# Layer 0's expert block in one order with the last units of its main attention

## What is computed

```python
x = x + gate_attn * attention(h)                  # main attention adds onto x, 256 tokens a unit
h = layernorm(x) * (1 + scale) + shift
inh = sigmoid(h @ Wr / temperature)               # 8 logits for each token
in_zone = (inh >= LO) & (inh <= 0.5)
distance = abs(inh - 1/e)
w  = exp(-distance / 0.1) * in_zone
fb = exp(-distance / 0.3) * top2_mask             # used where no expert is in the zone
weights = normalised(where(sum(w) < 1e-8, normalised(fb), w))
y = sum_e weights[:, e] * ((silu(h @ Wg[e]) * (h @ Wu[e])) @ Wd[e])
x = x + gate_ffn * y
```

## Time and profile before

| what | value |
|---|---|
| time, median of 3 runs | 1442.34 us (1441.42 to 1442.78) |
| the profiled execution's own time | 1450.17 us |
| its span, first to last instruction | 1448.0 us |
| mean granted TensorE clock | 0.951 of full speed |
| busy in the span: PE, DVE, ACT, POOL | 1313.8, 761.2, 761.9, 470.0 us |
| stretch from 828.6 to 1052.6 us: PE busy, granted clock | 180.02 of 224.00 us, 0.89 |
| first up product of the experts starts | 860.80 us |
| the four additions of one unit onto x; the statistics of four tiles behind them (DVE) | 1.66 us; 2.0 us (857.52 to 859.51 us) |
| from one expert's first up product to the next one's, experts 2 to 7 | 17.8 us |
| an expert's weights, issue to landing (768 KB) | 4.4 us |
| layer 1's attention weights (1024 KB): issue, time to landing | 875.35 us, 4.8 us |

### The profile page before, as it was taken

One profiled execution on the slowest core, in us unless ns is written; L12 is line 12 of the kernel. 1 busy time (PEld: TensorE's weight loads), 2 busy tenths in 40 slices (PEclk: granted clock), 3 DMA queues, 4 the chain that ended last, 5 costly groups with the idle time before them and its releaser, 6 DMA issues.

```text
span 1448.0 us, 21051 instructions
## 1 busy us (share of the span) xinstructions
PE 1313.8 (91%) x7838; PEld 884.5 (61%) x7838; DVE 761.2 (53%) x1233; ACT 761.9 (53%) x1424; POOL 470.0 (32%) x430
## 2 busy tenths in 40 slices
PE   6889999889999999999999867899658998779998
PEld 3633333347777776777777656788634444468997
DVE  4488877324454454454544634444337764354555
ACT  3457776655555555555555544233124767526553
POOL 4260054217465646555563002233300000013221
PEclk9989999999999999999999988899869999869999
DMA  7770000000000000000001011111037100011110
GB/s 274 182 174 1 1 16 8 9 0 23 15 15 15 16 23 11 19 16 23 8 23 52 1 44 43 38 45 44 1 92 166 25 1 1 1 48 52 46 43 30
DMA packets 27144, 59.57 MB, mean 41 GB/s; under 512 B 5986, under 2 KB 13410, under 8 KB 25954
## 3 DMA queue, kind: packets, MB, share of 16 engines
q1 hardware_dynamic: 27044, 58.24, 14.6%
HBM read 41.44 MB, written 8.39 MB: 34 GB/s over the span
## 4 chain that ended last, share of the span: by engine, by line
PE 81%; DVE 7%; ACT 5%; issue 3%; POOL 1%; DMA 1%; SPq 0%; ACTq 0%; DVEq 0%; POOLq 0%
PE bank L1525 8%; PE bank L1555 8%; PE bank L1237 7%; PE bank L1317 6%; PE bank L1771 6%; PE bank L1772 6%; PE bank L1773 6%; PE bank L1191 5%; PE bank L1492 4%; PE bank L1494 4%; PE bank L1493 4%; PE bank L1587 2%; DVE mpc L1133 2%; PE bank L1171 2%; ACT Pb L1217 2%
## 5 line engine op out<-in xcount | busy, mean ns | idle before, releaser
L1501 DVE TENSOR_REDUCE nmq<-bank 128x1 f32<-128x1024 f32 x128 | 156.5, 1223 | 253.1 <-PE bank L1494 253.0
L1217 ACT ACTIVATE Pb<-bank 128x512 f32<-128x512 f32 (+3 forms) x355 | 176.6, 576 | 57.9 <-PE bank L1191 40.7
L1073 DVE TENSOR_REDUCE mp<-bank 128x2 f32<-128x1024 f32 x128 | 153.3, 1221 | 46.2 <-PE bank L1065 46.0
L1516 ACT ACTIVATE Pq<-bank,nmq 128x1024 f32<-128x1024 f32 x127 | 141.4, 1113 | 45.8 <-DVE nmq L1501 45.7
L1525 PE MATMUL bank<-idf,Pq 128*128 128x128 f32 x1016 | 148.9, 278 | 5.5 <-ACT Pt4l L1538 5.1
L1525 PEld LDWEIGHTS bank<-idf,Pq 128*128 128x128 f32 x1016 | 117.4, 141 | 50.9 <-issue 17.9
L1538 ACT ACTIVATE Pt<-bank 128x512 f32<-128x512 f32 x187 | 110.5, 593 | 50.5 <-PE bank L1525 49.6
L1492 PE MATMUL bank<-qk1h,qk0h 128*128 128x512 f32 x256 | 121.0, 473 | 0.0
L1133 DVE TENSOR_REDUCE mpc<-bank 128x2 f32<-128x1024 f32 (+2 forms) x96 | 88.8, 954 | 55.8 <-PE bank L1124 35.0
L1555 PE MATMUL bank<-Pt,kvx 128*64 128x256 f32 x992 | 114.6, 383 | 0.0
L1950 POOL TENSOR_TENSOR hl<-hf,hh 128x512 fp32r<-128x512 f32 x32 | 41.3, 1290 | 194.9 <-ACT hh L1937 194.9
(11 more groups left out here) (336 smaller groups left out, 2914.2 us busy)
## 6 DMA issues: line engine op xcount, KB each, us to landing
t<-t SPq DMA_DIRECT2D x128, 64.0 KB, 2.0
wr<-wf SPq DMA_DIRECT2D x25, 256.0 KB, 2.6
wraw<-wf SPq DMA_DIRECT2D x8, 768.0 KB, 4.4
scratch<-stgr SPq DMA_DIRECT2D x4, 1024.0 KB, 4.0
scratch<-stg SPq DMA_DIRECT2D x8, 384.0 KB, 2.9
owT<-owT SPq DMA_DIRECT2D x1, 2048.0 KB, 9.9
qbn<-qbn SPq DMA_DIRECT2D x1, 1536.0 KB, 14.8
qstr<-scratch SPq DMA_DIRECT2D x6, 256.0 KB
```

Source lines behind the costliest of these rows:

```text
L1073: e.tensor_reduce(mp[:, w % 3, :, j, kh], wide[slot][:], AX, ALU.max).then_inc(ring_ok, 1)
L1217: e.activation(PBR[l][i % len(PBR[l])][:, 0:c], bank[b][:, 0:c], ACT.Exp, scale=0.25).then_inc(exp_ok[0], 1)
L1501: e.tensor_reduce(nmq[:, n % 8:n % 8 + 1], scores(u, i), AX, ALU.max, negate=True).then_inc(mp_ok, 1)
L1516: e.activation(probabilities(u, i)[:], scores(u, i), ACT.Exp, bias=nmq[:, n % 8:n % 8 + 1], accum_out=sums[:, u % 2, i:i + 1]).then_inc(ex ...
```

## The change

- `experts_order` is appended to `main_order`, so that each engine has one list for both; the four `..._experts0` functions are gone.
- A table `BESIDE_LAST` places the preparation in units 28 to 31. Expert 0's weights are split (up and down) at the end of unit 28, the statistics of the first half are taken in unit 30 behind transpose 6, the root in unit 31 behind transpose 1, the normalisation behind transpose 2, the turn and `hT` behind transpose 5, expert 1's splits behind transpose 7, and the first half's logits between `pv` 31 and `project` 31. The value product of unit 31 goes to bank 3.
- `hT` of the first half is written by DVE, and its `hTh` and `hTl` by POOL; of the second half `hT` is shared by ACT and DVE.
- The first up product waits no more for the last adds; the second one does. The second half is turned behind the third up product, its logits follow the fourth.
- The routing chain has 29 semaphore steps in place of 32, in five parts (`gating0`), with the exponentials of one part together; it runs beside the up products of experts 0, 1 and 2.
- Down products are two experts behind, with three buffers for `hh` and `hl`. Expert 2's up products stand without down products, then come expert 0's eight. The down split of an expert is asked for a whole expert ahead of its use.
- Layer 1's columns and gates come in expert 4, one piece at a time.
- At the end the down products of experts 6 and 7 alternate, and the addition onto x (`dve_onto_x`) runs one step behind.
- SP issues the weights of experts 0 to 3 ahead of `MAIN_DONE` (2 and 3 wait for the splits of 0 and 1).

The core of the diff:

```diff
+BESIDE_LAST = {
+    (28, 7): [("temperature",), ("wup", 0), ("wdown", 0)],
+    (30, 6): [("stats", 0)],
+    (31, 1): [("root", 0)],
+    (31, 2): [("normed", 0)],
+    (31, 5): [("turn", 0), ("hT", 0)],
+    (31, 7): [("wup", 1), ("wdown", 1)],
+    (31, "values"): [("logits", 0)],
+}
...
-        if u == 30:
-            order.append(("norm", 0))
...
-        if u == 31:
-            order.append(("norm", 1))
...
-    values(31)
+    order.extend([("pv", 31)] + BESIDE_LAST[31, "values"] + [("ot", 31)])
     output(31)
...
-    order = [("up", x, 0, m) for x in range(2) for m in range(2)] + [("second",)]
-    order += [("up", x, 1, m) for x in range(2) for m in range(2)]
-    order += [("down", 0, i) for i in range(NT)] + [("mod",)]
+    order = up(0, 0, 0)[:1] + [("stats", 1), ("root", 1)] + up(0, 0, 1)[:1] + up(0, 0, 0)[1:] + [("normed", 1)] + up(0, 0, 1)[1:]
+    order += up(1, 0, 0) + [("turn", 1), ("hT", 1)] + up(1, 0, 1) + [("logits", 1), ("gate", 0)]
+    order += up(0, 1, 0)[:1] + [("gate", 1)] + up(0, 1, 0)[1:] + up(0, 1, 1) + [("gate", 2), ("wup", 2)]
+    order += up(1, 1, 0) + [("gate", 3)] + up(1, 1, 1) + [("gate", 4)]
     for x in range(2, 8):
+        downs = [("down", x - 2, i) for i in range(8)] if x > 2 else []
         for half in range(2):
             for m in range(2):
-                order.append(("up", x, half, m))
-                order += [("down", x - 1, 4 * half + 2 * m + i) for i in range(2)]
-    return order + [("down", 7, i) for i in range(NT)]
+                order += up(x, half, m) + downs[:2 + x // 7]
+                del downs[:2 + x // 7]
+                if (half, m) == (0, 1) and x < 7:
+                    order.append(("wup", x + 1))
+                if (x, half, m) == (4, 0, 0):
+                    order.append(("columns",))
+                if x == 4 and half == 1:
+                    order.append(("shift_gate", m))
+                if x == 7 and (half, m) == (1, 0):
+                    order.append(("wdown", x))
+        if x == 2:
+            order += [("down", 0, i) for i in range(8)]
+        if x < 7:
+            order.append(("wdown", x))
+    for i in range(NT):
+        order += [("down", 6, i), ("down", 7, i)]
+        if i:
+            order.append(("onto_x", i - 1))
+    return order + [("onto_x", NT - 1)]
...
+    def dve_hT1(e, half, k):
+        e.wait_ge(ht_mm, 8 + 4 * half + 4)
+        e.tensor_scalar(hT[:, k, cols(half)], turn_bank(1, half, k)[:], modc[:, 0, 8 + k:9 + k], modc[:, 0, 6 + k:7 + k],
+                        ALU.mult, ALU.add).then_inc(hT_ok, 1)
+
+    def pool_hT1(e):
+        for k in range(2):
+            e.wait_ge(hT_ok, 4 + k + 1)
+            e.tensor_copy(hTh[:, k, 0:512], hT[:, k, 0:512]).then_inc(hTh_ok, 1)
+            e.wait_ge(hTh_ok, k + 1)
+            e.tensor_tensor(hTl[:, k, 0:512], hT[:, k, 0:512], hTh[:, k, 0:512].bitcast(F32),
+                            ALU.subtract).then_inc(hTl_ok, 1)
...
+        if half == 0:
+            e.wait_ge(d_f, 32)
...
+            e.wait_ge(pta_ok, 32 * (NT - len(BY_VECTOR)))
+            e.wait_ge(ptv_ok, 32 * len(BY_VECTOR))
+        e.wait_ge(hT_ok, 4 + 2 * half + 2)
...
+        elif i == 1:
+
+            e.wait_ge(*MAIN_DONE)
...
-        if x_ >= 2:
-            e.wait_ge(dn_mm, 8 * (x_ - 1))
-        e.activation(hh[x_ % 2][:, m, cols(half)], hf[:, n, :], ACT.Copy).then_inc(hh_ok, 1)
+        if x_ >= 3:
+            e.wait_ge(dn_mm, downs_done(x_ - 3))
+        e.activation(hh[x_ % 3][:, m, cols(half)], hf[:, n, :], ACT.Copy).then_inc(hh_ok, 1)
...
-        sp_expert0(e, 0)
-        sp_expert0(e, 1)
+        for x_ in range(4):
+            sp_expert0(e, x_)
         e.wait_ge(*MAIN_DONE)
```

More of the change, by code:

```diff
@@ L65, with up @@
 BY_VECTOR = (0, 6)
+def up(x, half, m):
+    return [("up", x, half, m), ("hidden", x, half, m)]
+BESIDE_LAST = {
[7 more added lines that the diff above has]
+}
 def main_order():
@@ L81, in turn @@
             order.extend(chunks.pop(0))
+        order.extend(BESIDE_LAST.get((u, k), ()))
     def score(u, i):
@@ L2075, in program, with pe_columns1, pe_gate1 @@
+    def pe_columns1(e):
+        b, free = OUTB["columns",]
+        e.wait_ge(*free)
+        e.wait_ge(d_moda, 32)
+        pe_columns(e, 1, (0, 6), b)
+    def pe_gate1(e, g):
+        b, free = OUTB["shift_gate", g]
+        e.wait_ge(*free)
+        pe_gate(e, 1, g, b)
     d_ew = [sem(f"d_ew{i}") for i in range(4)]
@@ L2431, in tensor @@
                 pe_cadd(e, s[1])
-            elif s == ("norm", 1):
+            elif s[0] == "turn":
                 e.wait_ge(exp_ok[1], 128)
-                pe_turn(e, 1, 0)
-        pe_experts0(e)
+                pe_turn(e, 1, s[1])
+            elif s[0] == "logits":
+                pe_logits0(e, s[1])
+            elif s[0] == "up":
+                pe_up0(e, *s[1:])
+            elif s[0] == "down":
+                pe_down0(e, *s[1:])
+            elif s[0] == "columns":
+                pe_columns1(e)
+            elif s[0] == "shift_gate":
+                pe_gate1(e, s[1])
         e.wait_ge(hf_ok, 32)
@@ L2622, in scalar @@
                 act_ctx(e, s[1])
-            elif s == ("norm", 0):
-                act_split_up(e, 0)
-                act_sd(e, 1, 0)
-            elif s == ("norm", 1):
-                act_hT(e, 1, 0)
-        act_experts0(e)
+            elif s[0] == "wup":
+                act_split_up(e, s[1])
+            elif s[0] == "wdown":
+                act_split_down(e, s[1])
+            elif s[0] == "root":
+                act_sd(e, 1, s[1])
+            elif s == ("hT", 1):
+                act_hT1(e)
+            elif s[0] == "hidden":
+                act_up0(e, *s[1:])
+            elif s[0] == "gate":
+                act_gating0(e, s[1])
         act_sd(e, 2, 0)
@@ L2681, in gpsimd @@
                 pool_product(e, p, k)
-        pool_experts0(e)
+        for s in MAIN:
+            if s[0] == "wdown":
+                pool_split_down(e, s[1])
+            elif s == ("hT", 0):
+                pool_hT1(e)
+            elif s[0] == "hidden":
+                pool_up0(e, *s[1:])
+            elif s[0] == "down" and s[1] == 7:
+                pool_gate0(e, s[2])
         e.wait_ge(a0_x, NT)
@@ L2735, in sync @@
         e.dma_start(bob[:], a["bo"].partition_broadcast(128)).then_inc(d_w1a, 16)
-        for x_ in range(2, 8):
+        for x_ in range(4, 8):
             sp_expert0(e, x_)
```

417 lines of the change are left out of this document (195 added, 222 removed).

## The result

The changed kernel takes 1396.99 us (median of 4 runs, 1394.14 to 1400.81), the kernel before 1442.56 us beside it (4 runs, 1441.42 to 1448.18): ratio 0.9678, 95% interval 0.9644 to 0.9713. That is 45.6 us less; the prediction said 43.5 less and 1399. The profiled execution is the one of 1394.14 us, with a span of 1392.2 us and a mean granted clock of 0.971 (0.951 before).

The account below looks back on a forecast made before the run. Attention's end and the expert block were taken as bound by PE's waits and the slow clock behind them. 160 + 10.4 + 4.4 + 1.5 + 4.2 made 180.5 us instead of 224, hence 1399 us, range 1389 to 1413.

Parts of the forecast that it names:

- PE's work up to the last up product: End of attention and expert block: PE's matmuls at full clock, 160 us in all including the last 16 down products.
- new waits: Units 30 and 31 and the restart: new PE idle time of 10.4 us, lower bound about 6, upper 18.
- columns followed by slow clock: Experts 3 to 7: layer 1's columns are followed by slow matmuls, as before the change; 1.5 us.
- from the last up product's end to the last statistics: Tail: 15.9 us, of which 11.5 already counted as 16 down products, so 4.4 extra.
- two slow stretches: Stretch with new waits close together: two runs of half-clock matmuls, about 2.1 us each, 4.2 in all.
- three collisions with POOL: Routing chain on DVE: one collision per part, costing PE 2.3, 1.8 and 1.7 us at up products 8, 9 and 10.
- Experts 3 to 7: Waits for POOL's down split go, PE should be full, an expert every 17.0 us in place of 17.8.
- The tail's step: Tail, each 128 tokens: two accumulations, an addition and statistics on DVE, 1.7 us where each took 2.1.
- The clock's rival: Restart: clock stays low, half of the first 12 up products slow, gain shrinks by 10 to 12, 1410 us; chance 0.15.
- The chain's: Restart: rival that the routing chain is the bound for longer, 18 us of new waits, 1406 us; chance 0.12.
- The good case: No slow stretch, and next stage's first projections at full clock; gain 50 us, 1392 us; chance 0.07.
- PE held at half clock: Experts 3 to 7: rival that PE without rests runs at half clock, making the kernel slower; chance 0.03.

Follow-up runs that it names:

- one_expert_behind: Changed kernel with down products one expert behind from expert 3 on, expert 0's and 1's both behind expert 2's up products; 1403.98 us, stage 193.47 us.
- changed_again: The changed kernel with no edit, run again on the same chip as later runs; 1398.38 us (5 runs), stage 187.88 us.
- kept_busy: Changed kernel plus 22 matmuls that nothing reads, between the last down product and the turn for layer 1; 1397.79 us.
- first_up_waits: Changed kernel with the first up product waiting for the last adds again; 1397.46 us, stage 189.49 us against 186.30.
- turned_by_act: Changed kernel with the first half's hT and hTh written by ACT again and hTl by DVE; 1401.04 us, stage 192.06 us.
- columns_in_halves: Changed kernel with layer 1's column products in two halves, behind expert 4's first and second up product; 1397.03 us (6 runs), stage 186.30 us.
- finer_and_columns: Changed kernel with the routing chain in ten parts, expert 2's weight split one up product later, and layer 1's columns halved; 1398.17 us (6 runs).

## Why the prediction was right

**The stretch.** In the prediction's own window, which begins 10.05 us into the stage, the sum said 176.3 us without the two slow stretches; it took 176.25. Term by term:

| term | predicted, us | measured, us |
|---|---|---|
| PE's work up to the last up product (160 less 16 down products) | 148.5 | 149.4 |
| new waits | 10.4 | 9.5 |
| columns followed by slow clock | 1.5 | 0 |
| from the last up product's end to the last statistics | 15.9 | 17.3 |
| two slow stretches | 4.2 | 0 |

The first and fourth are measured in these windows, cut at the end of the last up product:

```profile
823.23:982.14 158.91, 149.43 (x876) 126.36 (x875) 84.75 (x194) 61.52 (x100) 53.23 (x42) 1.00 0.13 44
...
982.14:999.48 17.34, 12.79 (x97) 11.65 (x95) 14.52 (x35) 2.52 (x3) 8.69 (x11) 0.93 0.01 1
```

The 10.4 us of new waits hold 0.1 us that the prediction's text doesn't explain. That 176.3 and 176.25 agree so closely is luck in part: the waits were 0.9 us shorter than said and the 1.5 us behind the columns did not come in this execution, while PE's work was 0.9 and the tail 1.4 longer.

**The waits** came one by one where they were put: transpose 1.1 (1.25 measured), `pv` 31 1.2 (1.44), third up product 1.1 (0.83), up product 6 1.1 (1.43), and 2.3, 1.8 and 1.7 at 8, 9 and 10 (1.98, 1.33, 1.23). The three collisions with POOL that I had assumed are the three in DVE's timeline above. The Trainium skill's rule on the shared port ("SBUF — State Buffer", section "Who interferes with whom") agrees with the 1.27 us row. DVE's split of expert 1's weights, for which the prediction allowed up to 1.3 us of delay, took 1.47 us where the split of expert 2's took 1.21. One reading of the old rows was off in its number only: the wait of 4.5 us in the earlier trace rows stands at up product 7 (900.07 us), not 6. Unit 28's end costs PE nothing, as taken: the timeline has no wait ahead of 824.88 us. The first up product came 19.2 us into the window; 848 less 828.6 made it 19.4.

**Table changes.** The row of 1.28 us held, not the 2.66 us of the Trainium skill ("ScalarE: Activation LUTs", section "What ACT_TABLE_LOAD costs"): in the changed kernel's timeline of ACT the silu starts 1.30 us after the load does.

```profile
861.94 1.28 ACT L2022 ACT_TABLE_LOAD   x1
863.24 0.60 ACT L2022 ACTIVATE sg<-bank 128x512 f32<-128x512 f32 x1
```

**Experts 3 to 7** have the period forecast, 16.85 us for 16.9; and the waits for POOL went, which `one_expert_behind` brought back.

**The tail's step** is 1.77 us for 1.7. The 1.4 us that this part took longer lie in that (0.5) and, for the most part, in its start: POOL finishes the last `hl` before it multiplies the first tile, and DVE's first addition waits 0.57 us for it and then takes 0.94.

**The slow clock** is the term that was mis-sized. I had taken two slow stretches and one behind the columns, 5.7 us, and the profiled execution had none, which is why the stage's gain is 47.7 and not 43.5. But that was that execution: `changed_again` has 1.6 us of it. In the median the gain was 45.6 us.

**The rivals.** The clock's rival (1410) fell: 0.99 in the stage. The chain's (1406) fell by size, 9.5 us and not 18; its mechanism is real, since DVE sets the pace of ups 8 to 10. The good case (1392) got its first half, no slow stretch. Its second didn't come: PE idles 5.73 us instead of 10.65 before layer 1's transposes, and the first projections still take 6.65 us (6.45 in the earlier trace rows); `kept_busy` shows that filling this gap doesn't bring the full clock for them either. PE held at half clock never appeared.

**How much each part is worth**, taken back alone: the preparation's place 7.3 us, two experts behind 7.2, the tail's delay 6.7, the first up product's early start 3.2, chain parts 2.7, the first half's turn on DVE and POOL 2.6. These add up to 29.7 of 47.7 us, each from one execution and without a test of whether they add. The rest was not taken apart: the order of the restart as a whole, the logits in two parts and the early weights. In the earlier trace rows three waits belong to it, 5.0, 4.1 and 3.2 us, and the changed kernel has none of them; that these and the slow matmuls behind them are the rest is argued, not shown.

## What to carry to other kernels

Where the waits of a full engine come from other engines' queues, price each moved instruction by the row of its kind and add up what stands in front of the one that is waited for: seven waits came out within 0.5 us each, and their sum within 1 us. An addition that needs another engine's result belongs one step behind it in the queue (6.7 us here, for a small change in the order). Before filling a waiting engine's gaps, look at who sets the pace there: extra work for PE bought 0.6 us, a shorter way through DVE's queue 2.8.

## What the runs showed of the hardware

- How long PE waits does not alone decide whether half clock follows. All waits of 3.2 us and more in the stage were followed by it. Waits of 1.85 us (`first_up_waits`) and 2.52 us (`turned_by_act`) were too, but not the one of 2.5 us at the same `pv` 31 in the kernel before; and the wait of 1.97 or 1.98 us at up product 8, which ten executions have, was followed by it in one (`columns_in_halves`), though not in the changed kernel with the same instructions around it.
- PE busy without a gap can fall to half clock as well: behind 3.6 us of one-column products, in 7 of 11 executions, for 1.5 to 3.2 us. In three of them the columns themselves took 4.56 to 4.80 us instead of 3.63.
- One program's executions on one chip are up to 19 us apart (`finer_and_columns`, 1391.86 to 1410.45 us). Of the longest, the trace shows a clock of 0.82 and 0.87 from 250 to 300 and 300 to 350 us, where the changed kernel's has 1.00 in both.
